# An attention and expert FFN kernel on one core: the up projection of token and expert blocks by seven products, and one normalisation on VectorE

## What is computed

```
x = x + quantised_mlp(layernorm(x), gate_up[b], ctx[b])      # per batch: int8-like smooth-quantised
                                                             # linear, silu(gate) * up, second linear
n = layernorm(x)                                             # 2048 tokens x 512
logits = n @ gate_w.T ; sel = the 2 of 8 experts with the largest sum of logits over all tokens
rw = softmax(logits[:, sel])
for k in (0, 1): h_k = gelu(n @ w1[sel_k] + b1[sel_k]) ; y_k = h_k @ w2[sel_k] + b2[sel_k]
x = x + sum_k rw[:, k] * y_k                                 # hidden width 2048
```

## Time and profile before

| what | value |
|---|---|
| median of the runs | 891.04 us (891.0 to 891.97) |
| the profiled execution | 887.1 us |
| its span | 885.3 us |
| TensorE's mean granted clock | 0.975 of full speed |
| PE, DVE, ACT, POOL busy | 93%, 42%, 35%, 12% of the span |

### The profile page before, as it was taken

The page is one execution under the profiler, slowest core; times in us unless marked ns, Lnnn a source line. Parts: engine busy times, 40 slices in busy tenths (PEclk is TensorE's granted clock), DMA queues, the critical chain, the costliest instruction groups (busy, mean ns, idle before and its releaser), DMA issues.

```text
span 885.3 us, 11147 instructions
## 1 busy us (share of the span) xinstructions
PE 825.6 (93%) x3767; PEld 661.9 (75%) x3767; DVE 373.9 (42%) x575; ACT 307.9 (35%) x532; POOL 102.8 (12%) x132
## 2 busy tenths in 40 slices
PE   3687877699999999999999999999999999999998
PEld 3565644388888888888888888888888888888886
DVE  2999997423333332333333323333333333334444
ACT  7975666422222222222222222222222222222221
POOL 1578884200000000000000000000000000000000
PEclk9798997899999999999999999999999999999999
DMA  9300000430000000000000000000000000000112
GB/s 347 129 1 1 1 1 0 144 96 24 24 24 25 24 24 24 24 24 24 24 24 24 24 24 24 24 24 24 24 24 24 24 1 0 0 1 1 47 47 95
DMA packets 27701, 32.29 MB, mean 36 GB/s; under 512 B 1400, under 2 KB 19864, under 8 KB 26784
## 3 DMA queue, kind: packets, MB, share of 16 engines
q1 hardware_dynamic: 27680, 32.02, 10.6%
HBM read 27.82 MB, written 4.19 MB: 36 GB/s over the span
## 4 chain that ended last, share of the span: by engine, by line
PE 82%; DVE 12%; DMA 2%; issue 1%; ACT 1%; SPq 1%; ACTq 0%; DVEq 0%
PE slot L638 40%; PE slot L624 39%; DVE rmax L910 3%; DVE peak_x L910 2%; DVE xv L960 2%; DMA wv<-in_fside_BxS2xS 2%; DVE stats L901 1%; DVE xv L973 1%; DVE wv L973 1%; PE slot L504 1%; DVE peak_a L910 1%; DVE scale L951 1%; DMA raw<-in_L_ffn_w 0%; PE slot L494 0%; DVE xt_lo L981 0%
## 5 line engine op out<-in xcount | busy, mean ns | idle before, releaser
L853 ACT ACTIVATE hid<-slot,b_col 128x512 f32<-128x512 f32 x128 | 88.0, 688 | 512.1 <-PE slot L624 511.6
L1120 DVE TENSOR_TENSOR h_lo<-hid,h_hi 128x512 fp32r<-128x512 f32 x128 | 88.4, 691 | 321.2 <-ACT h_hi L855 320.1
L624 PE MATMUL slot<-xt_hi,w_hi 128*128 (+1 forms) x512 | 203.1, 397 | 4.3 <-DVE w_lo L1012 4.3
L638 PE MATMUL slot<-w_hi,h_hi 128*128 128x512 f32 x512 | 203.5, 397 | 3.0 <-DVE h_lo L1120 3.0
L638 PE MATMUL slot<-w_hi,h_lo 128*128 128x512 f32 x512 | 201.9, 394 | 0.0
L624 PE MATMUL slot<-xt_hi,w_lo 128*128 (+1 forms) x512 | 201.4, 393 | 0.0
L624 PE MATMUL slot<-xt_lo,w_hi 128*128 (+1 forms) x512 | 200.5, 392 | 0.0
L638 PE MATMUL slot<-w_lo,h_hi 128*128 128x512 f32 x512 | 199.8, 390 | 0.0
L1146 DVE SCALAR_TENSOR_TENSOR res<-slot,rw,res 128x512 f32 x128 | 90.3, 751 | 139.0 <-PE slot L638 139.0
L624 PEld LDWEIGHTS slot<-xt_hi,w_hi 128*128 128x128 f32 x512 | 96.6, 189 | 25.1 <-DVE w_lo L1012 4.3
L638 PEld LDWEIGHTS slot<-w_hi,h_hi 128*128 128x128 f32 x512 | 96.4, 188 | 23.8 <-DVE h_lo L1120 3.4
(11 more groups left out here) (117 smaller groups left out, 555.9 us busy)
## 6 DMA issues: line engine op xcount, KB each, us to landing
raw<-in_L_ffn_w SPq DMA_DIRECT2D x64, 256.0 KB, 2.8
res<-in_x SPq DMA_DIRECT2D x4, 1024.0 KB, 9.3
wv<-in_fside_BxS2xS SPq DMA_DIRECT2D x4, 1024.0 KB, 15.0
out_x<-res SPq DMA_DIRECT2D x3, 1024.0 KB, 3.9
cv<-in_ctx SPq DMA_DIRECT2D x4, 512.0 KB, 11.4
out_x<-res SPq DMA_DIRECT2D x4, 256.0 KB, 2.7
b_row<-in_L_ffn_b SPq DMA_DIRECT2D x2, 256.0 KB, 4.4
b_rows<-in_L_ffn_b SPq DMA_DIRECT2D x2, 8.0 KB, 2.6
```

The costliest lines, as they stand in the source:

```text
L624: last = t.matmul(up_bank[f % 2][:, :], a[h][:, f, k, :], v[:, k, ds(at, T)], start=(n == 0), stop=(n == 3 * KD - 1))
L638: last = t.matmul(y_bank[j][:, :], a[f % 2][:, j * P:(j + 1) * P], v[h][:, f, :], start=(f == 0 and n == 0), stop=(f == FT - 1 and n == 2) ...
L853: s.activation(hid[f % 2][:, :], up_bank[f % 2][:, :], ACT.Gelu_apprx_tanh, bias=bias).then_inc(hid_ready, 1)
L1120: v.tensor_tensor(h_lo[f % 2][:, :], hid[f % 2][:, :], h_hi[f % 2][:, :].bitcast(F32), ALU.subtract).then_inc(h_ready, 1)
```

## The change

The tokens are taken in two pairs of batches (tp), the hidden columns in units of 256 (16 units, or pairs p, 8 of each expert). For a pair of batches and a unit the up projection is a 2x2 block product: the weights have blocks A11, A12, A21, A22 (128 hidden columns by 256 features), the activations B11 to B22 (256 features by 512 tokens). It is made by seven block products of sums of blocks in place of eight plain ones. The list of left factors is A_OF (S1 to S4 are sums of A blocks), that of right factors B_OF (T1 to T4 are sums of B blocks).

- PE: `strassen(p, tp, i, ...)` is one of the seven products, 6 matmuls. Products 0 and 2 accumulate in `x_bank`, 1, 3 and 5 in `p_bank`, 4 and 6 in `w_bank`. Behind the seven come four `down` of 12 matmuls as before.
- ACT copies product 0 to `e1`; DVE makes five `combine` adds of a bank and an SBUF tile between the products. One hidden tile is in `x_bank`, three are in SBUF (e3, e1, e2). ACT makes the gelus of all four.
- POOL makes the low parts of the hidden tiles (`hid_lo`), the sums of the next unit's weight blocks and the low parts of its weights; in the loop DVE no longer makes them. For the first unit DVE makes the sums and low parts (`first_weights`).
- POOL makes the sums of activation blocks, four of 128x1024 for each pair of batches (`operand_sums`), behind router 1 and behind router 3; ACT rounds them (`operand_hi`), DVE makes their low parts (`operand_lo`).
- ACT's `keep_hi` becomes `keep_block` for batches 0 to 2: the rounded copy and a full copy to SBUF, and the second one frees the slot. `keep_lo` reads the full copy instead of PSUM. Batch 3 has `keep_hi`, `last_lo` from PSUM, and `keep_full` behind them. Router 1 stands ahead of the transposes of batch 2.
- DVE's `normalise_last` makes the second normalisation of batch 3, four tensor_scalars, in place of ACT's `normalise(3, 2)`. `keep_lo(1, 1)` stands ahead of `moments(3, 2)`.
- All rows of b1 are loaded at the start, behind the gate weights on SP's queue, and transposed by PE; DVE's `pick_bias` selects by the one-hot masks. b2 is added two operations in each pass, at tp 1, behind the combines.
- Weights of w1 and w2 are loaded for 256 columns at a time, 512 KB each, and there is one set of rounded weights, refilled by product.
- Early tiles (xv, xq, wq) lie in the space of the operand tiles.

```diff
+def block_a(f, h):
+    return raw1[:, H * h:H * h + H, f * P:f * P + P]
+A11, A12, A21, A22 = block_a(0, 0), block_a(0, 1), block_a(1, 0), block_a(1, 1)
+S1, S2, S3, S4 = (ssum[:, i, :, :] for i in range(4))
+A_OF = (A11, S2, A12, S3, S1, A22, S4)
+T_ORDER = (1, 3, 4, 5)
+B_OF = ((B11H, B11L), (T2H, T2L), (B21H, B21L), (T3H, T3L), (T1H, T1L), (T4H, T4L), (B22H, B22L))
...
+    def load_w1(p):
+        sp.dma_start(raw1[:, :, :], w1_v[ds(expert[p // EP], 1), p % EP].rearrange("e p k f -> (e p) k f")
+                     ).then_inc(raw1_load, 16)
...
+    for p in range(1, PAIRS):
+        sp.wait_ge(a_ops_ready, 7 * p)
+        load_w1(p)
...
+    def operand_sums(tp, router_use):
+        even, odd = 2 * tp, 2 * tp + 1
+        slot_i, n = place(router_use)
+        kept(even, 0)
+        kept(odd, 0)
+        pool.wait_ge(filled[slot_i], n + 1)
+        g.tensor_tensor(part(tp, T1L), part(tp, T1H), part(tp, T2H), ALU.subtract).then_inc(tsum_ready[tp], 1)
+        kept(odd, 1)
+        pool.wait_ge(tsum_ready[tp], 1)
+        g.tensor_tensor(part(tp, T2L), part(tp, T3H), part(tp, T1L), ALU.subtract).then_inc(tsum_ready[tp], 1)
+        g.tensor_tensor(part(tp, T3L), part(tp, T3H), part(tp, T1H), ALU.subtract).then_inc(tsum_ready[tp], 1)
+        kept(even, 1)
+        pool.wait_ge(tsum_ready[tp], 2)
+        g.tensor_tensor(part(tp, T4L), part(tp, T4H), part(tp, T2L), ALU.subtract).then_inc(tsum_ready[tp], 1)
+    operand_sums(0, "r.1")
+    operand_sums(1, "r.3")
...
+    def hid_lo(p, tp, i):
+        pool.wait_ge(hid_ready, 8 + 8 * (2 * p + tp) + 2 * i + 2)
+        g.tensor_tensor(h_lo[:, i, :], hid[i][:, :], h_hi[:, i, :].bitcast(F32), ALU.subtract
...
+    def pair(p, final):
+        for i in range(4):
+            hid_lo(p, 0, i)
+        if not final:
+            weight_sums(p)
+            weight_lo(p, 0)
+        hid_lo(p, 1, 0)
+        if not final:
+            weight_lo(p, 1)
+            weight_lo(p, 2)
+        hid_lo(p, 1, 1)
+        hid_lo(p, 1, 2)
+        hid_lo(p, 1, 3)
+        if not final:
+            weight_lo(p, 3)
+            weight_lo(p, 4)
+            weight_lo(p, 5)
+            weight_lo(p, 6)
+            down_lo(p, 0, 1)
+            down_lo(p, 1, 0)
...
+    def strassen(p, tp, i, dst, start, first):
+        if tp == 0:
+            pe.wait_ge(a_ops_ready, 7 * p + i + 1)
+        if first and i in T_ORDER:
+            pe.wait_ge(t_ready[tp], T_ORDER.index(i) + 1)
+        hi, lo = B_OF[i]
         n = 0
-        for k in range(KD):
-            for a, v in ((w1_hi, xt_hi), (w1_hi, xt_lo), (w1_lo, xt_hi)):
-                last = t.matmul(up_bank[f % 2][:, :], a[h][:, f, k, :], v[:, k, ds(at, T)],
-                                start=(n == 0), stop=(n == 3 * KD - 1))
+        for k in range(H):
+            for a, v in ((a_hi, hi), (a_hi, lo), (a_lo, hi)):
+                last = t.matmul(dst, a[:, i, k, :], xo[tp][:, v, k, :], start=(start and n == 0),
+                                stop=(n == 3 * H - 1), skip_group_check=True)
                 n += 1
-        last.then_inc(up_ready, 1)
...
+    def pair(p, first, final):
+        for tp in range(2):
+            q = 2 * p + tp
+            pe.wait_ge(hid_ready, 8 * q + 2)
+            strassen(p, tp, 0, x_bank, True, first)
+            pe.wait_ge(comb_ready, 5 * q + 4)
+            strassen(p, tp, 1, p_bank, True, first)
+            pe.wait_ge(e1_ready, q + 1)
+            strassen(p, tp, 2, x_bank, False, first)
+            pe.wait_ge(comb_ready, 5 + 5 * q + 1)
+            strassen(p, tp, 3, p_bank, False, first)
+            pe.wait_ge(comb_ready, 5 * q + 5)
+            strassen(p, tp, 4, w_bank, True, first)
+            pe.wait_ge(comb_ready, 5 + 5 * q + 2)
+            strassen(p, tp, 5, p_bank, False, first)
+            pe.wait_ge(comb_ready, 5 + 5 * q + 3)
+            strassen(p, tp, 6, w_bank, False, first)
+            if tp == 0:
+                pe.wait_ge(w2_ready, 2 * p + 2)
+            down(p, tp, 0, 0, 0, True)
+            down(p, tp, 0, 2, 1, False)
+            last = down(p, tp, 1, 1, 1, True)
+            if tp == 1 and not final:
+                last.then_inc(w2_free, 1)
+            down(p, tp, 1, 3, 0, False)
...
+    def keep_block(b, h):
+        ps, empty = drain(f"y.{b}.{h}")
+        s.copy(xo[b // 2][:, HI_AT[b % 2][h], :, :], ps[:, :, :])
+        s.copy(part(b // 2, FULL_AT[b % 2][h]), ps[:, :, :].rearrange("p k t -> p (k t)")).then_inc(empty, 1)
...
+    def operand_hi(tp, at, sums):
+        hi, lo = at
+        act.wait_ge(tsum_ready[tp], sums)
+        s.copy(whole(tp, hi), part(tp, lo)).then_inc(thi_ready[tp], 1)
...
     normalise(1, 2)
-    keep_hi(1, 0)
-    keep_hi(1, 1)
+    keep_block(1, 0)
+    keep_block(1, 1)
     normalise(2, 2)
-    normalise(3, 2)
-    keep_hi(2, 0)
-    keep_hi(2, 1)
     keep_logits(1)
+    keep_block(2, 0)
+    keep_block(2, 1)
     keep_hi(3, 0)
     keep_hi(3, 1)
     keep_logits(2)
+    keep_full(3, 0)
     keep_logits(3)
...
+    def gelu(p, i, f, src):
+        bias = b1_now[:, f:f + 1]
+        s.activation(h_hi[:, i, :], src, ACT.Gelu_apprx_tanh, bias=bias).then_inc(hid_ready, 1)
+        s.activation(hid[i][:, :], src, ACT.Gelu_apprx_tanh, bias=bias).then_inc(hid_ready, 1)
...
+            if first and tp == 0:
+                act.wait_ge(b1_ready, 1)
+            if tp == 0:
+                s.copy(b1_now[:, :], b1_col[:, ds(2 * p, 2)]).then_inc(b1_ready, 1)
+                act.wait_ge(b1_ready, p + 2)
+            if refill:
+                act.wait_ge(sums_ready, 4 * p + 8)
+            next_hi(0)
+            act.wait_ge(prod_done, 7 * q + 3)
+            gelu(p, 0, 0, x_bank)
+            if first and tp == 0:
+                operand_hi(1, (T2H, T2L), 2)
+                operand_hi(1, (T3H, T3L), 3)
+            next_hi(1)
+            next_hi(2)
+            act.wait_ge(comb_ready, 5 + 5 * q + 3)
+            gelu(p, 1, 1, e3[:, :])
+            next_hi(3)
+            act.wait_ge(comb_ready, 5 + 5 * q + 4)
+            gelu(p, 2, 1, e1[:, :])
+            act.wait_ge(comb_ready, 5 + 5 * q + 5)
+            gelu(p, 3, 0, e2[:, :])
+            if first and tp == 0:
+                operand_hi(1, (T1H, T1L), 3)
+                operand_hi(1, (T4H, T4L), 4)
+            for i in (4, 5, 6):
...
-        v.tensor_tensor(xt_lo[:, H * h:H * h + H, b * T:b * T + T], ps[:, :, :],
-                        xt_hi[:, H * h:H * h + H, b * T:b * T + T].bitcast(F32), ALU.subtract
-                        ).then_inc(empty, 1)
+        emptied(f"y.{b}.{h}")
+        tp, p = b // 2, b % 2
+        v.tensor_tensor(whole(tp, LO_AT[p][h]), part(tp, FULL_AT[p][h]),
+                        whole(tp, HI_AT[p][h]).bitcast(F32), ALU.subtract).then_inc(lo_ready[b], 1)
...
+    def operand_lo(tp, n):
+        hi, lo = ((T2H, T2L), (T3H, T3L), (T1H, T1L), (T4H, T4L))[n]
+        dve.wait_ge(tsum_ready[tp], 4)
+        dve.wait_ge(thi_ready[tp], n + 1)
+        v.tensor_tensor(whole(tp, lo), part(tp, lo), whole(tp, hi).bitcast(F32), ALU.subtract
+                        ).then_inc(t_ready[tp], 1)
+    def normalise_last():
+        b = B - 1
+        dve.wait_ge(nmr_ready[b], 2)
+        for j in range(TT):
+            v.tensor_scalar(xv[b][:, j, :], res[:, b * TT + j, :], rstd[1][b][:, j:j + 1],
+                            nmr[1][b][:, j:j + 1], ALU.mult, ALU.add).then_inc(xn2_ready[b], 1)
...
+    def pick_bias():
+        rows_of = b1_all[:, :].rearrange("p (e u) -> p u e", e=E)
+        for k in range(TOPK):
+            link(v.tensor_tensor(picked[:, :, :], rows_of,
+                                 onehot[:, k:k + 1, :].to_broadcast([P, 2 * EP, E]), ALU.mult))
+            link(v.tensor_reduce(b1_col[:, 2 * k * EP:2 * (k + 1) * EP], picked[:, :, :], AX.X, ALU.add))
...
+    def first_weights():
+        dve.wait_ge(raw1_load, 16)
+        weight_lo(0)
+        weight_sum(1, S1, A21, A22, ALU.add)
+        weight_sum(2, S2, S1, A11, ALU.subtract)
+        weight_sum(3, S3, A11, A21, ALU.subtract)
+        weight_sum(4, S4, A12, S2, ALU.subtract)
+        weight_lo(1)
+        weight_lo(2)
+        operand_lo(0, 1)
+        weight_lo(3)
+        operand_lo(0, 2)
+        weight_lo(4)
+        operand_lo(0, 3)
+        weight_lo(5)
+        weight_lo(6)
...
+                            ).then_inc(w2_ready, 1)
     dve.sem_inc(y_free, TT)
     amax_w(0, 0)
@@ -1090,70 +1312,81 @@
     dequant(3, 2, 1)
     moments(2, 2)
     keep_lo(1, 0)
+    keep_lo(1, 1)
     moments(3, 2)
-    keep_lo(1, 1)
+    normalise_last()
     keep_lo(2, 0)
     keep_lo(2, 1)
...
+            def combine(dst, src, other):
+                v.tensor_tensor(dst[:, :], src, other[:, :], ALU.add).then_inc(comb_ready, 1)
+            dve.wait_ge(prod_done, 7 * q + 2)
+            dve.wait_ge(e1_ready, q + 1)
+            dve.wait_ge(h_ready, 4 + 4 * q)
+            combine(e2, p_bank, e1)
+            if first and tp == 0:
+                first_down_weights()
```

(36 more changed lines are left out.)

408 lines of the change are left out of this document (209 added, 199 removed), and 6 rows, old and new, of the table SLOT_USES.

## The result

The changed kernel takes **851.39 us** as the median of four runs (850.98 to 853.47), against 891.48 us (891.0 to 891.97) beside it: a ratio of 0.9555, 95% interval 0.9538 to 0.9572. It is 17 us faster than the forecast of 868.5, and 0.6 us under the low end of the range. The profiled execution took 851.66 us with a span of 849.9.

What follows compares the result with a forecast made beforehand. TensorE, busy for 93% of the span, bounds the kernel. Span 885.3 - 44.2 + 5.3 + 17.8 - 1.4 = 862.8 us, so 864.6 profiled and 868.5 median; own range 862 to 876, full range 852 to 879.

Steps and rivals of the forecast that it cites:

- 192 x 0.230: Up projection in the loop: 192 fewer matmuls at 0.230 us each, -44.2 us.
- Rival (4): Loop matmuls, with waits after every sixth, come at 0.238 instead of 0.230 us: 23 us, 891.5, no change; chance 0.03.
- The prologue: Ahead of the loop: first product at 184.0 us against 166.17, +17.8 us; bounds +3 and +23.
- rival (1): Prologue: the shared port doesn't cost it its rounds; loop starts at 169, 14.8 us less, 853.7; chance 0.20.
- (a) and (b): Prologue: one more DMA issued on SP, +0.5 us; ACT's two copies of each block, +0.9 us.
- Hand-overs in the loop: Between products, PE waits for copy e1 and combines: round trip 1.04 inside 1.15 us, cost 0, bound 10 us.
- (2): Loop: windows between products too short by 0.1 us, or the late hidden tile costs 0.9: +10, 878.5; chance 0.13.
- (3): Loop: POOL's port also holds the combines, 39 us more, 907, slower than before; chance 0.04.
- The stall of hidden tile 2: Loop, second token pair: POOL's low part waits for DVE's output bias add, PE stalls about 0.35 us; 15 pairs, +5.3 us.
- Start of the loop: First seven products wait for DVE's weights and operand_lo: 5.2 us lost against 6.6 before, -1.4 us; bounds 3 and 9 lost.
- Rival (5): End of prologue: POOL's power (lexp) holds the port; bias selection and first low part wait: +5.3, 873.8; chance 0.04.
- step (c): Prologue: keep_lo(1,0) and (1,1) take turns with POOL's powers; batch 3's shift-and-scale comes 2.4 us later, at 148.7.

Runs made afterwards that it cites:

- the second edit alone: Kernel before with only batch 3's second normalisation moved from ACT to DVE, four tensor_scalars behind moments(3, 2); ratio 1.0001 (0.9978 to 1.0024), the four take 1.92 us.

## Why the prediction missed

The forecast's difference of spans was -22.5 us and the measured one -35.4. Of the 12.9 us between them, 10.0 are one step. The other 4.2 us of the 17 by which the median was missed come from the step from the profiled execution to the median.

- **The step that failed: "192 x 0.230", with the 2880 matmuls that stay priced at their old distance.** The removed ones were right (192 x 0.2306 = 44.3). But 2880 x (230.56 - 227.1) ns = 10.0 us came off the rest. I took 0.230 from the earlier trace rows as a constant of this matmul. It was a property of where the kernel before had its tiles, and a change that lays out SBUF anew changes it. Padding that kernel by 320 bytes showed it directly: 11.9 us without one instruction changed. Against the padded kernel (879.81) the change gains 28, not 40. Rival (4), matmuls further apart, had this term with the wrong sign and the wrong cause.
- **The prologue: +17.8 was met by luck (+18.2 measured), and with it goes the step from the profiled execution to the median.** The steps named are there: four normalisations in 10.10 us (11.2 forecast), the two one-hots in 2.46, first low parts at 183.77; rival (1) is out. But two errors cancel. The shift of batch 3 (POOL's `nmr`), forecast for 148.7, or 150.1 with (a) and (b), was ready at 152.58; from there to the first product it took 31.8 us where the forecast had 33.9.
  The time up to the shift moves from execution to execution. In three profiles of kernels with the same prologue the shift ends at 146.34, 146.48 and 151.57, and the first up matmul stands at 166.17, 166.31 and 172.19. The execution shown of before was an early one (887.1, its median 891.04); the one of after lies 0.3 above its own median. I took those 3.9 us for a property of the kernel and added them: 4.2 us too much.
  By the medians the change gives 40 us, and the stretch from first up to last matmul gives 53.5, so the prologue costs some 14 us (an estimate). The term of +17.8 was about 4 too dear, and comparing an early execution with a usual one hid it. 2.1 of these 4 lie behind the shift, as above; where the rest lies is not shown.
- **Hand-overs in the loop: right.** Combines take 0.69 us as forecast, the products wait for DVE 1.1 us in all, and rivals (2) and (3) are out: all 160 combines, DVE's operations with one PSUM input, take 0.68 to 0.69 us, whatever POOL does beside them.
- **The stall of hidden tile 2: right in place and cause, half in size.** 5.3 us forecast for 15 pairs, 0.18 in each of 16 pairs and 2.8 us measured, with 3.1 regained when the b2 adds were moved. (By the forecast's own times, ready at 3.0 and wanted at 2.54, it would have been 0.46 a pair, and 0.16 with the port free; it put down 0.35 and 0.06.) The first b2 add (342.90 to 343.66) holds POOL's low part, which asked at 343.35, by 0.3 us, as worked out; but free of the port the low part is in time (no interval over 260 ns with the adds moved), where I had it 0.06 late already.
- **Start of the loop: right.** The first seven products and four down groups take 25.1 us where 90 matmuls at 227 ns take 20.4: 4.7 lost, 5.2 forecast.
- **Rival (5), out.** POOL's power does not hold the port. It ran 6.34 us from 181.17, and DVE's operations with two SBUF inputs didn't wait for it: the bias selection took 0.35, and a low part of 128x1024 took 1.22, beside the power (to 187.51) as behind it:

```profile
181.17 6.34 POOL L426 TENSOR_TENSOR lexp<-euler,lsub 128x32 f32<-128x32 f32 x1 [0.20 <-DVE lsub L1197]
182.15 0.35 DVE L1202 TENSOR_TENSOR picked<-b_all,onehot 128x128 f32<-128x128 f32 x1
...
186.62 1.22 DVE L1164 TENSOR_TENSOR xo<-xf,xo 128x1024 fp32r<-128x1024 f32 x1
...
188.09 1.22 DVE L1164 TENSOR_TENSOR xo<-xf,xo 128x1024 fp32r<-128x1024 f32 x1
```

The Trainium skill ("SBUF — State Buffer", section on SBUF's two separate sides) lets a GpSimd operation keep the shared port for the whole instruction. The sums agree: 10.10 us for four operations of 0.48. The power does not, and there the measurement decides. The other way round the power does wait. The one of batch 2 started 0.16 us behind DVE's two `keep_lo` (1.21 us each, two SBUF inputs) and was listed with 1.92; it took 1.01 for batch 3, and 1.02 for batch 2 in the kernel before, whose `keep_lo` reads PSUM:

```profile
145.96 1.92 POOL L317 TENSOR_TENSOR rstd<-var_e,neg_half 128x4 f32<-128x4 f32 x1
...
145.80 2.35 DVE L1150 TENSOR_TENSOR xo<-xf,xo 128x1024 fp32r<-128x1024 f32 x2
```

The same 0.9 us lie between 5.43 for the exponentials before and 6.34 here, where a low part ran from 181.01. So step (c) of the forecast had the right 2.4 for a wrong reason: the two `keep_lo` took no turns with a power, they take 2.35 us themselves, ahead of `moments`.

The range had its low end from rival (1) alone. No case allowed the matmuls to come closer together, though 2880 of them stood in the sum at a distance that only one layout had shown.

## What to carry to other kernels

A rate read from a full loop (here 0.2306 us a matmul) holds for that kernel's layout; before it is carried over, compare it with the lowest distance seen anywhere, and ask what could explain the rest. Give the tiles of weights and moving rows the same address modulo 256 bytes: it costs a pad of at most 255 bytes, and was worth 1.3% here. This was measured for fp32r weights of 128x128 against 512 columns alone. Take a time of a prologue from more than one execution. And where POOL makes long sums in SBUF, look at what DVE has to do beside them. Operations that read PSUM took their plain time, and so did reduces of an SBUF tile. Operations with two SBUF tiles waited, and so did tensor_scalars and a cast that read only one: the cast of the indices took 0.40 us beside a sum, until that sum ended at 173.87, and 0.17 without one (first line: changed kernel, second: kernel before with the second edit alone).

```profile
173.49 0.40 DVE L1186 CAST top_f<-top_i 128x8 f32<-128x8 uint32 x1
...
162.69 0.17 DVE L1003 CAST top_f<-top_i 128x8 f32<-128x8 uint32 x1
```

Each such operation can cost up to one whole POOL instruction.

## What the hardware showed that I had not expected

- The distance of 128x128 by 512 matmuls, each with its own weight load, depends on the byte address of the weights relative to the moving rows, modulo 256: 226.67 ns at 0 (544 cycles of 2.4 GHz at a granted clock of 1.00), 228.89 at 192, and 232.4 to 234.3 at 32 to 128. That is up to 3.4%, on an engine that is listed as busy all the time.
- After a stall, a matmul stream at distance 0 runs some ten uneven intervals (233, 236, 224, 231 ns and so on) before it is at 226.67 again. Shorter spells stand in the loop without a stall, too: with the b2 adds moved no interval is over 239 ns and the mean is 226.93. In the changed kernel both lift it to 227.1.
- POOL's power of 128x32 ran beside DVE operations with two SBUF inputs and held none of them, while its subtraction of 128x1024 held each for up to 2.35 us. A power that meets such a DVE operation already running is itself longer by 0.9 us (1.92 for 1.01, 6.34 for 5.43).
